# A different order of small work on the vector, scalar and sync engines in the first part of a four-stage transformer kernel

## The reference, cut to what matters

```
x = x + matmul(fake_quant(layernorm(x)), fake_quant(ctx))          # quantised product
x = x + (h @ W.T + b + 2 * lora(h, A, B, routing)),  h = layernorm(x)
        routing = softmax(mean over tokens 179..510 of h @ router_W.T + router_b)
x = x + attention(layernorm(x), ctx, ctx)    # 32 query heads, 8 key/value heads of 128, rope, softmax, wo
x = x + (h @ W_up.T + low_rank(h, top-1 expert)),    h = layernorm(x)
```

## Time and profile before

| | |
|---|---|
| median of 3 runs | 2017.83 us (2014.62 to 2019.3) |
| profiled execution | 2018.63 us, of which 2016.7 us is the span of the instructions |
| mean granted TensorE clock | 0.995 of full |
| PE busy | 1967.9 us (98%) |
| DVE, POOL, ACT busy | 1558.7, 1251.9, 1095.3 us |

### The profile page before, as it was taken

How to read it: one execution, slowest core, us unless ns; L and a number is a source line. 1 busy time by engine, 2 the same in 40 slices (tenths; PEclk the granted TensorE clock), 3 DMA queues, 4 the chain that set the end, 5 groups by cost and what they waited for, 6 DMA issues and landing times.

```text
span 2016.7 us, 26142 instructions
## 1 busy us (share of the span) xinstructions
PE 1967.9 (98%) x9140; PEld 1113.6 (55%) x9140; DVE 1558.7 (77%) x2703; ACT 1095.3 (54%) x1726; POOL 1251.9 (62%) x753
## 2 busy tenths in 40 slices
PE   8999999999979999999999999999999999999999
PEld 6876786878734444444444444444444444444587
DVE  5777697586788888788788889788888888888553
ACT  5453534436457565656656565665666656566310
POOL 1542353422068787878878788887867878786500
PEclk9999999999999999999999999999999999999999
DMA  7663546546899788877879699897877878778521
GB/s 261 198 212 97 173 146 209 179 141 226 262 218 195 149 180 149 183 162 157 178 144 189 147 221 207 201 212 169 179 159 147 183 147 175 163 155 164 148 77 69
DMA packets 673378, 349.54 MB, mean 173 GB/s; under 512 B 576768, under 2 KB 601600, under 8 KB 673248
## 3 DMA queue, kind: packets, MB, share of 16 engines
q1 hardware_dynamic: 673248, 347.87, 72.1%
HBM read 173.73 MB, written 31.46 MB: 102 GB/s over the span
## 4 chain that ended last, share of the span: by engine, by line
PE 74%; DVE 10%; DMA 2%; ACT 2%; issue 2%; POOL 2%; SPq 0%; ACTq 0%; DVEq 0%; POOLq 0%
PE ps L43 24%; PE ps L45 24%; PE ps L44 24%; DMA pT<-pp 1%; PE ps L922 1%; DVE psb L1745 1%; POOL u_sb L2256 1%; DVE pp L1760 1%; DVE t_sb L1305 1%; DVE t_sb L1307 1%; POOL ua L2309 1%; PE ps L929 0%; DVE ta L1292 0%; DVE tmp L1363 0%; DVE u_sb L1304 0%
## 5 line engine op out<-in xcount | busy, mean ns | idle before, releaser
L1745 DVE CUSTOM_DVE_ANT_0 psb<-ps,mask,sc 128x1024 f32<-128x1024 f32 x256 | 327.3, 1278 | 127.4 <-PE ps L45 127.2
L1760 DVE SCALAR_TENSOR_TENSOR pp<-psb,st,pp 128x1024 f16<-128x1024 f32 x256 | 364.0, 1422 | 47.4 <-ACT pp L2147 45.3
L2147 ACT ACTIVATE pp<-psb,st 128x1024 f16<-128x1024 f32 x256 | 293.2, 1145 | 176.5 <-DVE st L1755 121.8
L2140 ACT ACTIVATE psb<-psb,st 128x1024 f32<-128x1024 f32 x256 | 293.6, 1147 | 107.3 <-DVE st L1745 106.7
L2299 POOL TENSOR_SCALAR araw<-araw,kst 128x512 f32<-128x512 f32 x128 | 304.4, 2378 | 47.9 <-DMA araw<-in_wq 47.9
L2309 POOL TENSOR_TENSOR ua<-ua,ta 128x512 f32<-128x512 f32 x64 | 137.5, 2148 | 134.0 <-DVE ta L1292 134.0
L2299 POOL TENSOR_SCALAR araw<-araw,sc 128x512 f32<-128x512 f32 x128 | 215.6, 1684 | 3.0 <-DMA araw<-in_wo 3.0
L43 PE MATMUL ps<-pT,vsb 128*128 128x512 f16 x512 | 194.5, 380 | 8.1 <-DMA pT<-pp 8.1
L1774 DVE SCALAR_TENSOR_TENSOR x_lo<-ps,sc,x_lo 128x512 f32<-128x512 f32 x256 | 191.4, 748 | 13.5 <-PE ps L45 10.0
L43 PE MATMUL ps<-woh,osb 128*128 128x512 f16 x512 | 194.1, 379 | 5.7 <-DVE x_lo L1774 5.6
L2305 POOL TENSOR_TENSOR wol<-araw,woh 128x512 f16<-128x512 f32 x128 | 153.9, 1203 | 68.4 <-ACT woh L2079 68.3
(11 more groups left out here) (312 smaller groups left out, 3897.8 us busy)
## 6 DMA issues: line engine op xcount, KB each, us to landing
araw<-in_wq SPq DMA_DIRECT2D x128, 256.0 KB, 4.3
araw<-in_wo SPq DMA_DIRECT2D x128, 256.0 KB, 4.5
scan<-in_wq SPq DMA_DIRECT2D x64, 256.0 KB, 4.5
scan<-in_wo SPq DMA_DIRECT2D x64, 256.0 KB, 4.9
raw<-in_wv SPq DMA_DIRECT2D x16, 512.0 KB, 4.7
raw<-in_ctxT SPq DMA_DIRECT2D x16, 512.0 KB, 4.3
raw<-in_wk SPq DMA_DIRECT2D x16, 512.0 KB, 5.4
raw<-in_ctx SPq DMA_DIRECT2D x16, 512.0 KB, 4.5
```

What stands on the lines that cost most here:

```text
L1745: e.tensor_tensor_reduce(out=psb[:, n % 3, :], in0=pair(n % 2 * 2), in1=mask[:, i, :], scale=sc[:, 23 - H // 32:24 - H // 32], scalar=-LOW ...
L1760: e.scalar_tensor_tensor(out=pp[:, r, 1024:2048], in0=psb[:, r, :], scalar=st[:, n // 4 % 4, 16 + i:17 + i], in1=pp[:, r, 0:1024], op0=ALU ...
L2140: e.activation(P, P, ACT.Exp, bias=c[:, i:i + 1], scale=-1.0, accum_out=c[:, 8 + i:9 + i]).then_inc(a_exp.sem, 1)
L2147: e.activation(pp[:, r, 0:1024], psb[:, r, :], ACT.Copy, scale=st[:, n // 4 % 4, 16 + i:17 + i]).then_inc(a_ph.sem, 1)
```

## The change

Names of tiles are those of `RAW`. Nothing is computed that was not computed before, and no instruction is added but waits.

1. In `l0_end(0)`, DVE's low part of `w13` comes after the first operation of tile 1. It stood before `kv_end(23)`.
2. `sum_product(1)` and with it `table(1)` move from step 50/51 to 51/52.
3. At the change of batch, ACT and DVE split `c10` in step 30, ahead of `w17`. ACT does the square of `c9` behind `w17`, and splits `c12` in step 31, no longer in step 32.
4. A fourth landing buffer `raw4` lies over `junk` and its padding. `c20` and `w32` use it, `c20` is loaded in step 62 behind `c19`, and `c21`, `c22`, `c23`, `w33` move to other buffers.
5. DVE splits `c17` ahead of `kv_end(62)`. PE waits for `kv_end(62)` only at the second tile's group of k = 1.
6. DVE after step 63: `ffn_lo(2)` and `query_sums` come before `c22`, `row_sums(1)` after it. `query_scale` and `value_squares` come after `router_end(0)`.
7. `router_end(0)` writes bank 5 instead of 7. It waits for `v_h2[3]`, and `lora_t(0)` for `query_sums`; it no longer waits for DVE to read the router's bank.

```diff
-    "w28:0 w29:1 w30:0 c16:2 w31:1 c17:0 c18:2 c19:1 c20:0 c21:2 c22:1 c23:0 w32:2 w33:1"
+    "w28:0 w29:1 w30:0 c16:2 w31:1 c17:0 c18:2 c19:1 c20:3 c21:0 c22:2 c23:1 w32:3 w33:0"
-    SUM_AT = {21: 0, 50: 1}
+    SUM_AT = {21: 0, 51: 1}
@@ allocation, before junk
+    land = ExitStack()
+    raw4 = alloc(land, "raw4", [128, 1024])
+    land.close()
@@ sync_program
             if s == 62:
                 load_raw("c19")
+                e.wait_ge(a_kq.sem, a_kq.last)
+                load_raw("c20")
...
-        load_raw("c20")
         load_raw("c21")
@@ tensor_program, router_end and lora_t
             if b == 0:
-                e.wait_ge(v_ws.sem, v_ws["w", 0])
+                e.wait_ge(v_h2.sem, v_h2[3])
                 e.wait_ge(d_router.sem, d_router.last)
-                e.wait_ge(a_a1T.sem, a_a1T[7])
...
-                m = e.matmul(ps[:, 7 - b, 0:8], ...
+                m = e.matmul(ps[:, 5 + b, 0:8], ...
...
-                e.wait_ge(v_rt.sem, v_rt[0, 3])
+                e.wait_ge(v_ws.sem, v_ws["w", 0])
@@ tensor_program, chunks of W
-            if k == 1:
-                e.wait_ge(v_kr.sem, v_kr[62])
             for i in range(2):
+                if (k, i) == (1, 1):
+                    e.wait_ge(v_kr.sem, v_kr[62])
@@ vector_program
+                if (b, n) == (0, 1):
+                    split_lo("w13")
...
             elif s == 30:
                 kv_end(s)
                 split_lo("c9")
+                split_lo("c10")
             elif s == 31:
                 split_lo("w17")
-                split_lo("c10")
...
             elif s == 62:
+                split_lo("c17")
                 kv_end(s)
-                split_lo("c17")
                 split_lo("c18")
             else:
-                if s % 4 == 3:
+                if s % 4 == 3 and s + 1 not in L0_AT:
...
         split_lo("c21")
+        ffn_lo(2)
         query_sums()
-        query_scale()
+        split_lo("c22")
         row_sums(1)
-        ffn_lo(2)
-        split_lo("c22")
...
         ffn_norm(4)
+        router_end(0)
+        query_scale()
         value_squares()
-        router_end(0)
@@ scalar_program
             elif s == 30:
                 split_hi("c9")
+                split_hi("c10")
             elif s == 31:
                 split_hi("w17")
-                split_hi("c10")
+                key_square(("c", 9))
                 split_hi("c11")
+                split_hi("c12")
```

More of the change, by code:

```diff
@@ L63 @@
 RAW_BEFORE = {}
-for _slot in range(3):
+for _slot in range(4):
     _in = [key for key in RAW_ORDER if RAW_SLOT[key] == _slot]
@@ L68 @@
     ["w0", "c0", "c1", "w1", "c2", "c3", "c4", "c5", "c6", "c7"] + [f"w{n}" for n in range(2, 17)]
-    + ["c8", "c9", "w17", "c10", "c11", "c12", "c13", "c14", "c15"] + [f"w{n}" for n in range(18, 27)]
+    + ["c8", "c9", "c10", "w17", "c11", "c12", "c13", "c14", "c15"] + [f"w{n}" for n in range(18, 27)]
     + ["c16", "w27", "w28", "w29", "w30", "w31", "c17", "c18", "c19", "c20", "c21", "c22", "c23", "w32", "w33"]
@@ L311, in split_dst, with raw_at @@
         return (wl if hl else wh)[:, n % 2, :]
+    def raw_at(key):
+        return raw[:, RAW_SLOT[key], :] if RAW_SLOT[key] < 3 else raw4[:, :]
     def raw_src(key):
@@ L570, in load_raw @@
             r = RAW_SLOT[key]
-            e.dma_start(raw[:, r, :], raw_src(key)).then_inc(d_raw[r].sem, 16)
+            e.dma_start(raw_at(key), raw_src(key)).then_inc(d_raw[r].sem, 16)
         def load(name, dst):
@@ L973, in router_end @@
             for k in range(8):
-                m = e.matmul(ps[:, 7 - b, 0:8], temp(("r", b))[:, k * 128:k * 128 + 128], small[:, 64 + k * 8:72 + k * 8],
+                m = e.matmul(ps[:, 5 + b, 0:8], temp(("r", b))[:, k * 128:k * 128 + 128], small[:, 64 + k * 8:72 + k * 8],
                              start=k == 0, stop=k == 7)
@@ L1295, in split_lo @@
             e.wait_ge(a_hi.sem, a_hi[key])
-            tt(split_dst(key, 1), raw[:, RAW_SLOT[key], :], f32(split_dst(key, 0)), ALU.subtract).then_inc(v_lo.sem, 1)
+            tt(split_dst(key, 1), raw_at(key), f32(split_dst(key, 0)), ALU.subtract).then_inc(v_lo.sem, 1)
         def rope(src, cos, sin, u, t):
@@ L1496, in router_end @@
             e.wait_ge(t_rt.sem, t_rt[b])
-            e.scalar_tensor_tensor(out=small[:, 16:24], in0=ps[:, 7 - b, 0:8], scalar=1.0 / 332.0, in1=small[:, 40:48],
+            e.scalar_tensor_tensor(out=small[:, 16:24], in0=ps[:, 5 + b, 0:8], scalar=1.0 / 332.0, in1=small[:, 40:48],
                                    op0=ALU.mult, op1=ALU.add).then_inc(v_rt.sem, 1)
@@ L1900, in split_hi @@
                 e.wait_ge(t_kv.sem, t_kv[(31, n - 9) if n < 16 else 31 if n == 16 else (63, n - 17)])
-            e.copy(split_dst(key, 0), raw[:, r, :]).then_inc(a_hi.sem, 1)
+            e.copy(split_dst(key, 0), raw_at(key)).then_inc(a_hi.sem, 1)
         def kv_end(s):
@@ L2247, in split_lo @@
             e.wait_ge(a_hi.sem, a_hi[key])
-            e.tensor_tensor(split_dst(key, 1), raw[:, RAW_SLOT[key], :], f32(split_dst(key, 0)),
+            e.tensor_tensor(split_dst(key, 1), raw_at(key), f32(split_dst(key, 0)),
                             ALU.subtract).then_inc(p_lo.sem, 1)
```

7 lines of the change are left out of this document (3 added, 4 removed).

## The result

The changed kernel takes 2006.01 us (median of 4 runs, 2005.41 to 2009.67). The kernel before, beside it, took 2017.91 (4 runs, 2014.62 to 2019.30). The ratio is 0.9947, 95% interval 0.9932 to 0.9962, so 8 to 14 us were gained. Measured once more, in another set of runs, it was 2009.86 (6 runs) against 2017.41 (11), ratio 0.9955 [0.9937, 0.9973]. The forecast was 2006.2 us.

A forecast was written before the change was run, and what follows sets the result against it. PE was taken to bound the kernel, busy 1967.9 of 2016.7 us. Gains of 3.7 (w13), 1.4 (sum product), 2.2 (change of batch) and 4.3 (W's chunks to router) summed to 11.6 us, forecasting 2006.2 us, range 2002 to 2014.

The forecast's parts named there:

- The ceiling: Most the change could give back: PE's idle time 12.97 us plus clock losses 1.56 and 1.6, 16.1 us in all.
- the nine waits: PE's idle gaps from the first quantised product to the end of `router_end(0)`, 12.97 us in sum.
- The two gaps of 0.5 and 0.75: First quantised product: PE idle times in us expected in place of its 3.38 us wait.
- rival (b): `w13`, `c10`, `w17`, `c19` each wait for a whole 1.2 us POOL operation on the shared port; 2009.8 us, chance 0.10.
- The 0.28 and the 1.14: Change of batch: PE waits in us, the latter for `c12`, expected to go.
- The wait of 0.8 at c22: End of the second batch: a PE wait of 0.8 us expected to remain at `c22`.
- The cover of 1.3 us at `lora_scale`: After LoRA's product: DVE expected done at 452.3, 1.3 us before PE asks at 453.6.
- the sign of being wrong: PE waiting at `ffn_end(0)`, named beforehand as one of the signs that the forecast is wrong.
- rival (a): DVE's `lora_scale` or evictions come late, so the gain from `c17` through the router is given back; 2010.5 us, chance 0.15.
- (c): Attention's first heads: more DMA-transpose stalls of 7.0 us each; 2013.2 us with one, 2020.2 with two; chance 0.10.
- (d): Moved tiles do not move their waits, so only `c12` and router edits may pay, 4.4 us; 2013.4 us, chance 0.05.
- the two falls of the clock: Slow PE clock in the first quantised product, 1.56 us lost, and behind the router wait, 1.6 us lost; both expected back.

The follow-up runs named there:

- n5_h_lo: Changed kernel with DVE's `h_lo(7)` moved ahead of `scale_mask(0, 1)` and `scores_max(0)` at the attention's start; 2009.71 us, ratio to before 0.9958.
- n3_c19: Changed kernel with ACT splitting `c19` and `c20` in step 62 ahead of its key copy, loads of `c21` to `c23` ahead of a store; 2007.01 us, ratio 0.9942.
- a_after: The changed kernel measured and profiled again, nothing further edited; 2009.86 us, ratio to before 0.9955.
- n4_all: Changed kernel with `w17` ahead of `c10` again, `c19` and `c20` split earlier on ACT, `query_scale` and `value_squares` behind `lora_scale(0)`; 2003.95 us, ratio to before 0.9931.
- e4_router: Kernel before with only the router in bank 5 and LoRA's product not waiting for DVE to read it; 2015.4 us, ratio 0.9987.
- e1: Kernel before with only `w13`'s low part moved among the evictions; 2015.31 us, ratio 0.9988.
- e3: Kernel before with only the change of batch edited: `c10` ahead of `w17`, `c12` split a step early, square of `c9` later; 2017.96 us in one run.
- e6: Kernel before with only DVE's order after step 63 changed, router still in bank 7; 2015.56 us, ratio 0.9990.
- e5_chunks: Kernel before with only the fourth landing buffer, `c17` ahead of `kv_end(62)` and PE's later wait for that key copy; 2014.49 us in one run.

## Why the prediction was right

The sum was forecast at 11.6 us and measured, over A, B, C, E and F, at 10.6 and 10.8. From the first quantised product's start to the feed-forward stage's end (A to G) before took 404.67 us, the changed kernel 393.32 and 394.15. That end came at 541.38 us where 539.5 was forecast; 1.33 of the 1.9 between were there before anything changed was reached. By steps:

**The ceiling.** PE's idle time and its clock were the bulk of it. The 16.1 left out the 0.25 us that a wait costs besides: five of the nine waits stand between matmuls of three-part products at full clock, 1.2 us. One term has a slip: 7.4 - 5.3 - 0.4 is 1.7 and not 1.6. Nothing that DVE, ACT or POOL did elsewhere moved a stretch clear of its spread, but for H in the first profile.

**Item 1**: 3.7 forecast, 3.57 and 3.55 measured in the full change, 3.2 alone. The two gaps of 0.5 and 0.75 came out at 0.42 and 0.95. w13's low part did meet POOL, in the profile after 1.83 us on DVE beside 1.16 on POOL:

```profile
154.96 1.83 DVE L1298 TENSOR_TENSOR wl<-raw,wh 128x1024 fp32r<-128x1024 f32 x1
```
```profile
154.56 1.16 POOL L2267 TENSOR_TENSOR khl<-u_sb,khl 128x512 f16<-128x512 f32 x1 [0.73 <-ACT khl L1917]
```

POOL is through at 155.72 and DVE ends 1.07 us later. By the rule of the Trainium skill's page SBUF — State Buffer, section "SBUF: two separate sides", DVE would stand still for the whole rest of POOL's operation. The trace agrees within 0.16 us: 0.76 us were left of it, and the low part took 0.60 longer than the 1.23 without a meeting. So this meeting cost what was left of POOL's operation, and not the 1.2 that rival (b) charged.

It can cost that much. n5_h_lo has the changed kernel's code here, yet its A is 27.57, 1.3 us above after. DVE's 128x4 operation ahead of the first eviction took 1.33 us there, 0.23 in after:

```profile
153.02 1.33 DVE L1436 TENSOR_SCALAR small<-small,scal 128x4 f32<-128x4 f32 x1
```
```profile
153.07 1.26 POOL L2265 TENSOR_TENSOR u_sb<-u_sb,t_sb 128x512 f32<-128x512 f32 x1 [0.57 <-DVE t_sb L1313]
```

PE's waits in the first product were then 1.44, 0.34 and 0.56 us. The gain of item 1 is 2.2 us by this profile.

**Item 2**: 1.4 forecast, 1.50 and 1.74.

**Item 3**: 2.2 forecast, 1.82 and 1.98, alone 1.96. The 0.28 and the 1.14 went as worked out. The wait at w17 stayed at 1.90 where 1.5 were forecast. This low part met POOL as well, 1.85 us beside 1.68, but 0.6 us for that were in the forecast. What it had wrong is ACT's copy. It was to start 1.6 us before PE runs out of work and started 1.1 before (209.67, PE idle from 210.80), because c10's copy is now ahead of it and had itself waited for its landing, and behind that stood a key copy:

```profile
210.75 1.85 DVE L1298 TENSOR_TENSOR wl<-raw,wh 128x1024 fp32r<-128x1024 f32 x1 [0.25 <-ACT wh L1909]
```
```profile
208.19 1.05 ACT L1909 CAST slots<-raw 128x1024 fp32r<-128x1024 f32 x1 [1.48 <-DMA raw<-in_ctxT]
...
209.67 1.05 ACT L1909 CAST wh<-raw 128x1024 fp32r<-128x1024 f32 x1
```
```profile
209.84 1.68 POOL L2267 TENSOR_TENSOR khl<-u_sb,khl 128x512 f16<-128x512 f32 x1 [1.89 <-ACT khl L1917]
```

**Items 4 and 5**: 0.4 forecast, 0.2 alone. That the key chain behind `kv_end(62)` sets c19 and c20 was right (forecast waits 0.7 and 1.2, measured 0.73 and 1.12), and n3_c19 shows the converse. What had to be moved was ACT's copies ahead of the key copy in that chain, with the loads behind them, and that is worth 2.7 to 2.9 us.

**Item 6**: E fell by 1.39 and 1.20 in the whole change where 1.25 were forecast, the 0.4 of items 4 and 5 included. The wait of 0.8 at c22 did not come. It was 0.14 in after and 0.32 in a_after.

**Item 7**: 3.0 forecast and 3.15 alone, but 2.35 in the whole change. This is the term that was mis-sized. The cover of 1.3 us at `lora_scale` was not there. The profile after has the wait of 0.51 at `ffn_end(0)`, which the prediction had named as the sign of being wrong. DVE's rows of after show why, with POOL's residual addition beside both:

```profile
437.79 1.35 DVE L1513 CUSTOM_DVE_ANT_0 small<-small 128x8 f32<-128x8 f32 x1
...
445.04 0.74 DVE L1523 TENSOR_SCALAR u_sb<-ps,small 128x512 f32<-128x512 f32 x1
446.48 1.68 DVE L1298 TENSOR_TENSOR ts_sb<-u_sb,ts_sb 128x512 fp32r<-128x512 f32 x1 [0.69 <-ACT ts_sb L1977]
```
```profile
436.72 2.40 POOL L2284 TENSOR_TENSOR x_hi<-x_hi,ctab 128x1024 f32<-128x1024 f32 x1 [22.16 <-DVE tmp L1369]
445.21 2.40 POOL L2284 TENSOR_TENSOR x_hi<-x_hi,ctab 128x1024 f32<-128x1024 f32 x1 [6.09 <-DVE tmp L1369]
```

I had counted on `value_squares` shrinking because POOL would be done, and so it did (0.17 us in place of 2.33). But POOL's addition, which no longer finds it, meets what DVE has there now: the 128x8 operation of `router_end` took 1.35 us, 0.15 in before. The next addition met the low part of `lora_scale`, 1.68 us where before had 0.69. Together that is 2.2 us against a cover of 1.3, and 0.5 us of it reached PE as a wait. `query_scale` itself took the 1.9 us forecast (it is nine operations and `query_sums` three, not fifteen in all). `query_scale` behind `lora_scale` takes the wait away (F 22.25 in n4_all, as in e4_router, where `query_scale` never stood in between). So 0.8 us were lost to rival (a) in small.

**Rivals.** (a) is that 0.8 us and no more. (b) happened at w13 and w17 at half its price, and in n5_h_lo, at another operation of item 1, at its full price. (c), one more stall of 7.0 us in the attention, did not come in either profile. But H and I together were 57.07 and 57.39 us, 1.5 and 1.8 more than before (55.58); kernels with nothing edited there go from 55.13 to 57.32, so this is not clear of the spread. (d) is refuted by e1, e3 and e6, each of which paid alone; for items 4 and 5 it was right.

**What rests on luck.** I took the two falls of the clock for certain; by the windows they came in five of the six profiles that have the first wait and five of six that have a wait behind the router. So some 3 of the 10.6 us are gained in most executions but not in all. The two measured ratios, 0.9947 and 0.9955, lie within each other's intervals. That 2006.2 met the first median within 0.2 us is luck too: the profiled execution was forecast at 2007.0 and took 2009.67, the second median is 3.7 us higher, and the sum of the stretches is 0.8 to 1.0 us under the forecast sum.

## What to carry to other kernels

Follow a wait back until you reach an engine that was itself idle, and move what stands at that point: a fourth buffer and an earlier low part of c17 gave 0.2 us, ACT's copies ahead of the one that waited for POOL, with the loads behind them, gave 2.7 to 2.9. Charge a wait with its idle time, with 0.25 us on top (this kernel's matmuls), with the clock that may fall behind it, and with nothing of these if a later wait would absorb it. A small DVE operation can be a large risk beside POOL: look for it wherever POOL has a long operation that the same event releases.

## What was unexpected of the hardware

- The idle time alone does not tell whether the clock falls. It fell to 0.50 behind 0.46 us after the router's 8-column matmuls (e6_order). It stayed at 1.00 behind 1.90 us (after) and once behind 3.15 us (e5_chunks), and fell to 0.50 behind 2.23 us (n3_c19), at a place where 2.29 and 2.47 us left it up (e4_router, e6_order). Behind the same 2.6 us at 500 to 510 it fell in a_after and stayed up in after.
- One fall costs 1.3 to 1.8 us where PE sets the pace (e5_chunks against the others), and about 0.7 where a wait follows.
- An operation of 128x8 elements on DVE took 1.35 us beside POOL's 128x1024 addition, and one of 128x4 took 1.33 beside its 128x512 addition (n5_h_lo). Not every small one is held up: beside the same 128x1024 addition a reduction, a multiplication of 128x1 and a reciprocal took 0.16, 0.15 and 0.17 us.
- A wait of PE costs more than its idle time at a granted clock of 1.00: 0.23 to 0.28 us between the matmuls of the first part, 0.14 to 0.16 in the attention.
